# Where the last layer's expert results are stored from, and when TensorE reads the expert's number

## The reference

```python
B, S, D, F, E = (4, 512, 256, 128, 64)          # TOPK = 8 experts of 64 for each row
topk_w, topk_idx = _route(x, w_router, b_router)
idx_flat = topk_idx.reshape(-1)
sort = jnp.argsort(idx_flat)
tok = sort // TOPK
x_sorted = x_flat[tok]
group_sizes = jnp.bincount(idx_flat, length=e).astype(jnp.int32)
g = jax.lax.ragged_dot(x_sorted, we_gate, group_sizes)
u = jax.lax.ragged_dot(x_sorted, we_up, group_sizes)
o = jax.lax.ragged_dot(jax.nn.silu(g) * u, we_down, group_sizes)
y = jnp.zeros_like(x_flat).at[tok].add(o * w_sorted[:, None])
return y + shared                                # shared: one more gated product for all rows
```

## Time and profile before

| | |
|---|---|
| median of three runs | 2326.88 us (2324.38 to 2330.84) |
| the profiled execution | 2326.39 us |
| its span, first to last instruction | 2324.7 us |
| TensorE busy | 1861.1 us, 80% of the span |
| VectorE, GpSimd, ScalarE busy | 67%, 54%, 45% |
| share of the chain that ended last on SyncE's queue (SPq) | 10% |

### The profile page before, as it was taken

The page is one execution under the profiler, slowest core; times in us unless marked ns, Lnnn a source line. Parts: engine busy times, 40 slices in busy tenths (PEclk is TensorE's granted clock), DMA queues, the critical chain, the costliest instruction groups (busy, mean ns, idle before and its releaser), DMA issues. The chain is left out here.

```text
span 2324.7 us, 38548 instructions
## 1 busy us (share of the span) xinstructions
PE 1861.1 (80%) x11288; PEld 1296.8 (56%) x11289; DVE 1551.5 (67%) x3374; ACT 1037.6 (45%) x2965; POOL 1261.1 (54%) x1015
## 2 busy tenths in 40 slices
PE   6799968989898668999869999699727999999100
PEld 6478833343433243677648888588512888888000
DVE  7699829999999968333447777377688333333733
ACT  1576637666666323233157777343306333333000
POOL 2588617777777700788425555366101555554776
PEclk9699988999999977999989999899765999999555
DMA  9121013212121052899601110100411999998333
GB/s 288 35 95 53 8 51 129 97 49 92 55 88 58 0 171 60 224 296 253 153 10 37 33 34 25 30 2 2 144 51 37 284 288 283 285 283 272 109 116 103
DMA packets 163806, 272.06 MB, mean 117 GB/s; under 512 B 28722, under 2 KB 97300, under 8 KB 162708
## 3 DMA queue, kind: packets, MB, share of 16 engines
q1 hardware_dynamic: 130708, 199.72, 26.6%
q0 software_dynamic: 30464, 68.19, 11.3%
q10 hardware_dynamic: 2496, 2.44, 0.3%
HBM read 218.74 MB, written 51.53 MB: 116 GB/s over the span
## 5 line engine op out<-in xcount | busy, mean ns | idle before, releaser
L1009 POOL TENSOR_TENSOR b_h<-b_h,b_bcb 128x1024 f32<-128x1024 f32 x128 | 301.7, 2358 | 115.4 <-DVE b_h L1074 114.9
L1588 POOL DMA_INDIRECT m1x_xb<-scratch_xn,m_tok x192 | 182.4, 950 | 313.8 <-DVE m1x_yb L1785 157.1
L1074 DVE TENSOR_TENSOR_SCAN b_h<-b_dA,b_pbx 128x1024 f32<-128x1024 f32 x128 | 292.6, 2286 | 4.4
L822 PE MATMUL b_psy<-b_h,ident 128*128 128x512 f32 x512 | 247.1, 611 | 55.9 <-POOL b_h L1009 55.9
L1635 PE MATMUL m1x_psh<-m1x_xe,m1x_w 128*128 128x128 f32 x1536 | 209.0, 280 | 7.5 <-DMA m1x_w<-in_m_w 6.7
L822 PEld LDWEIGHTS b_psy<-b_h,ident 128*128 128x128 f32 x512 | 93.5, 192 | 191.5 <-POOL b_h L1009 104.2
L1772 DVE TENSOR_TENSOR m1x_hT<-m1x_sg,m1x_psh 128x128 f32<-128x128 f32 x192 | 55.3, 288 | 215.6 <-ACT m1x_sg L1722 215.6
L1635 PEld LDWEIGHTS m1x_psh<-m1x_xe,m1x_w 128*128 128x128 f32 x1536 | 188.1, 193 | 16.8 <-issue 11.6
L1958 POOL TENSOR_TENSOR x_s<-x_s,x_rs 128x1024 f32<-128x1024 f32 x64 | 121.1, 1893 | 126.5 <-DVE x_rs L2124 126.5
L956 ACT ACTIVATE b_dA<-b_delta,b_A 128x504 f32<-128x504 f32 x256 | 166.1, 705 | 52.4 <-DVE b_h L1074 49.9
L1068 DVE TENSOR_TENSOR b_pbx<-b_pdx,b_bcb 128x1024 f32<-128x1024 f32 x128 | 157.7, 1232 | 21.7 <-ACT b_pdx L939 15.0
(11 more groups left out here) (456 smaller groups left out, 4436.4 us busy)
## 6 DMA issues: line engine op xcount, KB each, us to landing
m1x_w<-in_m_w SPq DMA_DIRECT2D x192, 256.0 KB, 4.3
b_bcb<-scratch_bc_rows SPq DMA_DIRECT2D x64, 512.0 KB, 4.6
scratch_y<-m1x_yb SPq DMA_DIRECT2D x192, 128.0 KB, 3.9
m_w<-in_m_w SPq DMA_DIRECT2D x64, 368.0 KB, 4.0
a_c<-in_ctxT SPq DMA_DIRECT2D x16, 512.0 KB, 4.3
m_w<-in_m_w SPq DMA_DIRECT2D x64, 128.0 KB, 4.1
x_area<-in_ctxT SPq DMA_DIRECT2D x32, 256.0 KB, 2.6
m_w2all<-in_m_w SPq DMA_DIRECT2D x1, 8192.0 KB
```

What stands on the lines that cost most here:

```text
L822: mm = pe.matmul(psy[:, k % 2, :], ident[:, :], h[:, u % HB, j, :], start=False, stop=(nq == NQ - 1 and j == CQ - 1))
L1009: q.tensor_tensor(hs, hs, bcb[:, 1, CQ * nq:CQ * nq + CQ], ALU.mult).then_inc(sem("hc"), 1)
L1074: v.tensor_tensor_scan(h[:, u % HB].rearrange("p j n -> p (j n)"), dA[:, u % DB].rearrange("p j n -> p (j n)"), pbx[:, :, :].rearrange("p ...
L1588: g.indirect_dma_start(out=xb[:, j, :], out_offset=None, in_=xn, in_offset=bass.IndirectOffsetOnAxis(ap=tok[:, b:b + 1], axis=0)).then_inc ...
```

## The change

The stores leave SyncE's program. ScalarE gets them as a fourth part of its steps, with an empty third place between, so that it stores block b in the step in which it does `rows` of b + 3 and `gate` of b + 2. TensorE's `output` reads the expert number before it waits for `hT` and `yb`, no longer between the waits and the product.

```diff
@@ SyncE
-                    def store(p, j):
-                        sp.wait_ge(xs("yb", j % 2), used(p, j) + 1)
-                        sp.dma_start(y.rearrange("(b p) d -> b p d", p=P)[bass.ds(R * p + j, 1)].rearrange("o p d -> (o p) d"), yb[:, j, :]).then_inc(xs("y_stored", j), 16)
...
                             weights(p + 1, j)
-                            if not capped:
-                                store(p, j)
-                    for j in () if capped else range(R):
-                        store(NR - 1, j)
@@ TensorE, output(p, j)
                         u = j % 2
+                        if not capped:
+                            b = pe.value_load(ebrow[0:1, bass.ds(R * p + j, 1)], min_val=0, max_val=E - 1)
                         pe.wait_ge(xs("hT", u), used(p, j) + 1)
                         pe.wait_ge(xs("yb", u), used(p, j))
...
                         else:
-                            b = pe.value_load(ebrow[0:1, bass.ds(R * p + j, 1)], min_val=0, max_val=E - 1)
                             mm = pe.matmul(psyy[u][:, 0:D], hT[:, u, 0, :], w2all[:, bass.ds(b, 1), :].rearrange("p o d -> p (o d)"), start=True, stop=True)
@@ ScalarE
+                    def store(p, j):
+                        a.wait_ge(xs("yb", j % 2), used(p, j) + 1)
+                        a.dma_start(y.rearrange("(b p) d -> b p d", p=P)[bass.ds(R * p + j, 1)].rearrange("o p d -> (o p) d"), yb[:, j, :]).then_inc(xs("y_stored", j), 16)
...
-                    in_steps(a, [rows, gate], NR, R)
+                    in_steps(a, [rows, gate] if capped else [rows, gate, None, store], NR, R)
```

## The result

The changed kernel takes 2272.86 us (2269.98 to 2275.57), the kernel before on the same chip 2328.18; the ratio is 0.9767, 95% interval 0.9751 to 0.9783. That is 55 us less.

What follows compares the result with a forecast made beforehand. SyncE's issue work, 1.849 us a block, was taken as the bound. With 186 steps at 1.61 instead of 1.819 saving 38.8 us, and 0.6 at the end, 39.4 less than 2326.39 gave 2287, range 2279 to 2307.

Steps and rivals of the forecast that it cites:

- some 50: Sign on SyncE's queue: it waits for TensorE's `output` in nearly every block, together some 50 us.
- Rival 4: ScalarE becomes the bound through the store ahead of `rows`: 1.95 us a block, 24 us slower, 2351; chance 0.03.
- Rival 2: TensorE's read of the expert number isn't covered: blocks at 1.745 us, 13.8 us less, 2313; chance 0.07.
- Rival 3: No change: the DMA engines give no more than 284 GB/s, blocks stay at 1.82 us, 2326; chance 0.03.
- the term of the block's time: Blocks 4 to 190: 186 steps at 1.61 us in place of 1.819, 38.8 us less.
- The cap by the DMA engines: In the blocks, a highest share of 1.06, 326 GB/s, holds a step at 1.61 us where TensorE needs 1.59.
- Rival 1: DMA engines bound the blocks clearly above 1.61: steps of 1.66 to 1.76 us, 2296 to 2315; chance 0.26.
- The round's end: `turn` follows `output` after 0.59 instead of 0.32 us there: 0.27 / 8 = 0.03 a block for TensorE's array.
- TensorE's own step: The array's need from one `output` to the next when nothing is late: 1.56 us.
- 2278: Fast end of the forecast's steps, 1.56 us each: 48.8 us less, reached only if rounds' ends cost nothing.
- 525 KB a block: What the DMA engines must carry for each block: weights, gather and store; 1.61 us at 326 GB/s.
- The end of the blocks: Last block: the 0.76 us of issue ahead of the last product nearly goes, 0.6 us saved once.

Runs made afterwards that it cites:

- B: The kind of chip (5, 6 and 9) on which the kernel before takes 2340 to 2342 us; the changed kernel there took 2333.66, ratio 0.9969.
- the half output: The changed kernel computing only 128 of the output product's 256 columns, copied out twice, all bytes still moved: 2336.49 us (0.9985), on another chip 2248.62 (0.9650).
- two steps behind: The changed kernel without ScalarE's empty place, so the store of block b stands behind `gate` of b + 1: 2350.94 us (1.0036), again 2350.19 (1.0046).
- A: The kind of chip on which the kernel before takes 2328 to 2330 us; the changed kernel there took 2272.86 (0.9767) and 2271.88 (0.9752).
- two behind turned round: The changed kernel without ScalarE's empty place, and VectorE copying to `yb` of block b before making `hT` of b + 1: 2314.46 us (0.9888).

## Why the prediction was wrong in size

**What held.** SyncE's issue work was the bound and left the chain; it waits 51 us, as forecast ("some 50"), though in 153 blocks and not in nearly every one. The store costs ScalarE 0.34 us, stands behind `gate`, and `rows` keeps 0.85 us of cover. The number is read before `hT` is there. Rival 4 (ScalarE the bound) was off: it takes two issues a store to bring it on, and then at 1.63. (That all issues but one are at 0.31 to 0.53 holds for the rows shown; ahead of the blocks ScalarE has one of 0.57 and SyncE one of 2.8.) Rival 2 (the read not covered) didn't come, but its mechanism shows where the store moves alone: 1.71 to 1.72 on B, near its 1.745. Rival 3, no change, fell: the store alone gave 22, 25 and 30 us on three chips. The rule of the Trainium skill's page "DMA: Bandwidth & Descriptors", section "Issuing engines are not separate DMA queues", was rightly not followed: all it leaves to be gained is the issuing sequencer's time. That is small beside the transfer here too, 0.54 us against landings of about 4, and yet it was the bound.

**The step that failed** is the term of the block's time, 1.61 in the prediction and 1.545 in the trace; over 186 steps that is the 12.2 us by which blocks 4 to 190 gained more (51.0 against 38.8). It has three parts of 11.9 us in all; the small rest is the step to block 190, which took 1.32.

- *The cap by the DMA engines*, 1.61 for TensorE's 1.59: 186 x 0.02 = 3.7 us. I took the share at 283 GB/s, 0.92, as proportional to the rate, and 1.06 as the highest, 326 GB/s. Measured: 341 at 1.00, and 373 at 1.04 with the output product halved. The share is a poor gauge of what is left, since the same bytes took less engine time when they moved faster: over blocks 4 to 190 it is 0.324 per 100 GB/s before, 0.31 with the store alone (B), 0.295 in the changed kernel and 0.279 in the half output. Nor was the 1.06 a limit for this mix. In that stretch, 860 to 880 us, one queue alone had it (packets, MB, share of 16 engines), while in the changed kernel's blocks three share the engines:

```profile
q1 hardware_dynamic: 4566, 6.60, 105.6%
```

  Rival 1, built on the same scale, fell with it.
- *The round's end*, 0.03 a block: 5.6 us. I carried the 0.27 of the earlier trace rows over as a need of TensorE's array. It is its sequencer's branch and register work, and is hidden once the sequencer runs ahead, which the early read lets it do: in the changed kernel `turn` follows `output` after 0.33 at the rounds' ends too, while with the store alone it is still 0.59. It stays at 0.59 wherever something else leaves TensorE waiting (two steps behind, the read alone), and comes back where the array's work shrinks: in the half output most steps are 1.33 to 1.34 and one in each round 1.75 to 1.83.
- *TensorE's own step*, 1.56 read from the earlier trace rows, measured 1.546: 2.6 us. The 0.91 from `hidden` to `output` in the step with nothing late was still 0.02 too long, the rest of the read.

The prediction gave 2278 as the time if the rounds' ends cost nothing, and left it out of its range. They did cost nothing, and with steps of 1.545 the loop by itself brings 2326.9 down to 2274.9. (Its 525 KB a block are 524, which changes nothing.) The end of the blocks was mis-sized the other way: from the last but one `output` to the last it was 1.45 before and is 1.04, 0.4 gained in place of 0.6. The whole loop went from 346.5 us to 294.5, 52.0 less, in both traces of the changed kernel. The medians differ by 55 and 58. In the first pair of traces the spans differ by 56.5: 52.0 in the loop, 5.2 ahead of it and 0.7 the other way behind it. What lies ahead is chance, since executions of one kernel begin the loop up to 5 us apart, and so is a part of how far the time fell below the range.

**Was it two parts or one?** On A the changed kernel's pace is the array's. The store alone leaves 0.157 a block of uncovered read, 29 us; the read alone gives nothing. So the read's part is worth about 29 of the 52, and only with the store. That is an estimate: neither half ran on A, and it rests on the store-only trace of chip 9.

**What stays open.** Why SyncE is held, and what waits for TensorE starts late, on chips of kind B; whether the pace brings it on or TensorE's read among the products of `hidden`; and what such a chip has that the others don't. The run meant to tell pace and read apart fell on the other kind. Nor was the kernel before traced on B. Of its 13 us more some 7 lie behind the blocks in all traces of B; if the other 6 lie in them, its pace there is about 1.819 + 6 / 186 = 1.85, under the 1.87 to 1.89 of the read alone. That is an estimate. The prediction gave no chance to a result that depends on the chip.

No complete kernel that ran on A beats the changed one there. On B the store alone does, by 22 us on the same chip, and two behind turned round has as good a ratio (0.989); on A the store alone should cost 29. The changed kernel ran on one chip of kind B.

## What to carry to other kernels

When an engine's chain is nothing but its own issues, count its issue work against the compute engine's own step, and move issues until the compute engine is the slower. Then bound the new pace by the array's own products, spaced as in a step where nothing is late, and treat branches and register work as hidden if the sequencer gets ahead. Don't cap the rate by a DMA share measured at another rate. Give a store that moves to a compute engine such a place that the copy it waits for was made a step earlier: one empty step was worth the whole gain here. And measure on more than one chip.

## What was not expected of the hardware

- The DMA engines carried 373 GB/s at a share of 1.04 in this mix of a 256 KB load, an indirect gather and a store, and 341 at 1.00, where the earlier trace rows have 331 at 1.06.
- On chips of kind B, SyncE's instructions are held for up to 0.7 us and `gate` starts up to 3 us after the products it needs, above all in kernels that would run at 1.55 and below. It turns a gain of 55 us into one of 8. On those of kind A an instruction was held once in eight traces.
- Reads of a number into a register took 0.27 us on SyncE and 0.30 to 0.32 on TensorE at the median, and cost TensorE 0.157 a block only where they stood behind its wait.
